# A three-term float32 product x + T[k] x: unit 0 in three pieces, the first x's fourth tile on SyncE's queue, new orders at the start

## The reference

```python
x:    (8, 512, 512)      # b, j, k
T:    (100, 512, 512)    # t, i, j
itok: (8,) int32         # 1 .. 98
Tb = T[itok - 1]
out = x + jnp.einsum('bij,bjk->bik', Tb, x)
```

## Time and profile before

| | us |
|---|---|
| median of three runs | 103.97 (103.88 to 104.11) |
| profiled execution | 104.08 |
| its span, first to last instruction | 102.3 |
| TensorE busy in the span | 96.1 (94%) |
| VectorE, GpSimd, ScalarE busy | 86.9, 72.7, 65.1 |
| matmuls of the three products (L452, L463, L474), each group | 34.5, 34.4, 33.2 |

### The profile page before, as it was taken

The page is one execution under the profiler, slowest core; times in us unless marked ns, Lnnn a source line. Parts: engine busy times, 40 slices in busy tenths (PEclk is TensorE's granted clock), DMA queues, the critical chain, the costliest instruction groups (busy, mean ns, idle before and its releaser), DMA issues.

```text
span 102.3 us, 1825 instructions
## 1 busy us (share of the span) xinstructions
PE 96.1 (94%) x440; PEld 80.1 (78%) x440; DVE 86.9 (85%) x100; ACT 65.1 (64%) x86; POOL 72.7 (71%) x38
## 2 busy tenths in 40 slices
PE   4996999999999999999999999999999999999950
PEld 4994888868888888888888888888888888888840
DVE  0165888999999999999999999999999999993250
ACT  0764669659578685858585859587785858452110
POOL 2000459999989799897979797979798998908100
PEclk9999999999999999999999999999999999999997
DMA  1899998996989889896999889998999330405064
GB/s 47 307 201 401 366 236 205 389 310 167 322 293 307 302 253 379 231 343 146 324 351 326 190 287 331 327 275 263 349 248 313 129 146 13 192 0 208 6 272 139
DMA packets 20749, 25.30 MB, mean 247 GB/s; under 512 B 2306, under 2 KB 16898, under 8 KB 19970
## 3 DMA queue, kind: packets, MB, share of 16 engines
q10 hardware_dynamic: 3602, 15.34, 41.7%
q1 hardware_dynamic: 17136, 9.84, 36.2%
HBM read 16.78 MB, written 8.39 MB: 246 GB/s over the span
## 4 chain that ended last, share of the span: by engine, by line
PE 88%; DMA 5%; SPq 2%; issue 0%; DVE 0%; ACT 0%
PE same L452 29%; PE same L463 28%; PE diff L474 28%; DMA T_sb<-T 5%; PE turned L437 1%; SPq L169 1%; PE diff L484 1%; PE turned L426 1%; PE same L484 0%; SPq L155 0%; DVE out_sb L409 0%; ACT TH_r L225 0%
## 5 line engine op out<-in xcount | busy, mean ns | idle before, releaser
L301 POOL TENSOR_TENSOR xL<-x_sb,xH 128x1024 fp32r<-128x1024 f32 x14 | 33.8, 2412 | 7.6 <-ACT xH L210 7.6
L317 POOL TENSOR_TENSOR TD_r<-TH_r,TL 128x1024 fp32r<-128x1024 f32 x14 | 33.8, 2413 | 2.9 <-issue 2.9
L452 PE MATMUL same<-xH,TH_r 128*128 128x512 f32 x128 | 34.5, 391 | 0.2 <-ACT TH_r L225 0.2
L463 PE MATMUL same<-xL,TL 128*128 128x512 f32 x128 | 34.4, 391 | 0.0
L474 PE MATMUL diff<-xD,TD_r 128*128 128x512 f32 x124 | 33.2, 390 | 0.1
L246 ACT ACTIVATE diff<-same 128x512 f32<-128x512 f32 x31 | 18.1, 582 | 22.8 <-PE same L463 22.8
L357 DVE STREAM_TRANSPOSE turned<-T_sb 128x512 f32<-128x512 f32 x28 | 29.2, 1089 | 0.0
L452 PEld LDWEIGHTS same<-xH,TH_r 128*128 128x128 f32 x128 | 23.9, 188 | 5.3 <-ACT TH_r L225 0.4
L463 PEld LDWEIGHTS same<-xL,TL 128*128 128x128 f32 x128 | 23.9, 188 | 4.9
L474 PEld LDWEIGHTS diff<-xD,TD_r 128*128 128x128 f32 x124 | 23.2, 188 | 5.2 <-issue 0.5
L385 DVE TENSOR_TENSOR out_sb<-x_sb,diff 128x512 f32<-128x512 f32 x31 | 20.9, 675 | 4.7 <-PE diff L474 4.7
(11 more groups left out here) (25 smaller groups left out, 21.6 us busy)
## 6 DMA issues: line engine op xcount, KB each, us to landing
out<-out_sb ACTq DMA_DIRECT2D x15, 512.0 KB, 5.2
T_sb<-T SPq DMA_DIRECT2D x112, 64.0 KB, 4.0
x_sb<-x ACTq DMA_DIRECT2D x6, 1024.0 KB, 6.6
x_sb<-x SPq DMA_DIRECT2D x2, 512.0 KB, 7.8
x_sb<-x ACTq DMA_DIRECT2D x2, 256.0 KB, 3.5
x_sb<-x ACTq DMA_DIRECT2D x1, 512.0 KB, 4.6
T_sb<-T SPq DMA_DIRECT2D x2, 256.0 KB, 5.6
T_sb<-T SPq DMA_DIRECT2D x1, 512.0 KB, 6.4
```

The source lines that it names most:

```text
L301: nc.gpsimd.tensor_tensor(half(xL, h), x_sb[b % X_SLOTS][:, i:i + 2], half(xH, h).bitcast(fp32), ALU.subtract).then_inc(xL_ready, 2)
L317: nc.gpsimd.tensor_tensor(TD_r[s][:], TH_r[s][:].bitcast(fp32), TL[s][:].bitcast(fp32), ALU.subtract).then_inc(TD_ready, 2)
L452: nc.tensor.matmul(same[U % 2][:], TH_r[p][:, i, j], xH[s][:, j], start=(j == 0), stop=False)
L463: done = nc.tensor.matmul(same[U % 2][:], TL[p][:, i, j], xL[s][:, j], start=False, stop=(j == N - 1))
```

## The change

Unit 0's transposed T, which stood in two pieces of two blocks (each with its own TH and TL cut), stands in three: block 0, block 1 and blocks 2 and 3. Block 1's piece goes into a free quarter of the bank `same[1]`. The first x is loaded in four transfers of one tile each instead of three; tiles 0 to 2 by ScalarE as before, and tile 3 by SyncE, behind T0 and ahead of T1. ScalarE cuts tile 3 behind the T cuts of unit 0, VectorE takes its low part behind the TL cuts. TensorE does unit 0's high and low products of blocks 0 to 2 around turn(1), and then the high and the low product with tile 3. Besides, ScalarE cuts half 2 of x before cut_T(3) instead of after it, VectorE's transposes of units 4 and 5 come before cut_T(3) and before sum_up(0), where they stood after sum_up(0), and WARM is 8 instead of 10.

```diff
--- before.py
+++ after.py
@@ -27,8 +27,7 @@
     RADIX = 4096.0
     LEAN = 1.0 - 0.5 / RADIX
     BY_PE = N
-    FIRST_X = [(0, 1), (1, 2), (2, 4)]
-    WARM = 10
+    WARM = 8
     HALVES = [slice(0, D // 2), slice(D // 2, D)]
 
     x_part = x.rearrange("b (p u) k -> b p u k", u=N)
@@ -61,20 +60,21 @@
         same = [ps(f"same{i}", [P, D]) for i in range(2)]
         diff = [ps(f"diff{i}", [P, D]) for i in range(2)]
 
-        first_halves = [(turned[:, 0, 0:2], slice(0, 2)), (turned[:, 1, 2:4], slice(2, 4))]
+        first_pieces = [(turned[:, 0, 0:1], slice(0, 1)), (same[1][:, P:2 * P].rearrange("p (j i) -> p j i", j=1), slice(1, 2)),
+                        (turned[:, 1, 2:4], slice(2, 4))]
 
         last_diff = [diff[(UNITS - 1) % 2], same[UNITS % 2]]
 
         eye_step = sem("eye_step")
         itok_loaded = sem("itok_loaded")
         x_loaded = [sem(f"x_loaded{s}") for s in range(X_SLOTS)]
-        first_x_loaded = [sem(f"first_x_loaded{i}") for i in range(len(FIRST_X))]
+        first_x_loaded = [sem(f"first_x_loaded{u}") for u in range(N)]
         half_x_loaded = [sem(f"half_x_loaded{i}") for i in range(2)]
         T_loaded = [[sem(f"T_loaded{s}_{n}") for n in range(N)] for s in range(T_SLOTS)]
         turned_by_pe = sem("turned_by_pe")
         turned_by_dve = sem("turned_by_dve")
-        first_half_turned = sem("first_half_turned")
-        first_half_TH_ready = sem("first_half_TH_ready")
+        first_piece_turned = sem("first_piece_turned")
+        first_TH_ready = sem("first_TH_ready")
         TH_ready = sem("TH_ready")
         TL_ready = sem("TL_ready")
         TD_ready = sem("TD_ready")
@@ -142,6 +142,9 @@
         def load_x(eng, b):
             eng.dma_start(x_sb[b % X_SLOTS][:], x_part[b]).then_inc(x_loaded[b % X_SLOTS], 16)
 
+        def load_first_x(eng, u):
+            eng.dma_start(x_sb[0][:, u], x_part[0, :, u]).then_inc(first_x_loaded[u], 16)
+
         def load_second_x(eng, i):
 
             eng.dma_start(x_sb[1][:, 2 * i:2 * i + 2], x_part[1, :, 2 * i:2 * i + 2]).then_inc(half_x_loaded[i], 16)
@@ -173,7 +176,9 @@
                 return sp.snap(t, min_val=0, max_val=K - 1)
 
             t = matrix(itok_row[0:1, 0:1])
-            load_T(sp, t, 0)
+            load_T(sp, t, 0, range(1))
+            load_first_x(sp, N - 1)
+            load_T(sp, t, 0, range(1, N))
             load_second_x(sp, 0)
             load_second_x(sp, 1)
             sp.wait_ge(itok_loaded, 16)
@@ -194,7 +199,7 @@
         @block.scalar
         def _(act):
             def cut_first_x(u):
-                act.wait_ge(first_x_loaded[min(u, 2)], 16)
+                act.wait_ge(first_x_loaded[u], 16)
                 nc.scalar.activation(xH[0][:, u], x_sb[0][:, u], COPY, scale=LEAN).then_inc(xH_ready, 1)
 
             def cut_x_half(h):
@@ -216,13 +221,13 @@
                 nc.scalar.activation(xH_copy[:], half(xH, h).bitcast(fp32), COPY).then_inc(xH_copied, 1)
 
             def cut_first_T():
-                for i, ready in enumerate((first_half_TH_ready, TH_ready)):
-                    bank, blocks = first_halves[i]
-                    if i == 0:
-                        act.wait_ge(first_half_turned, 1)
+                for i, (bank, blocks) in enumerate(first_pieces):
+                    if i < 2:
+                        act.wait_ge(first_piece_turned, i + 1)
                     else:
                         wait_turned(act, 1)
-                    nc.scalar.activation(TH_r[0][:, 0, blocks], bank, COPY, scale=LEAN / RADIX).then_inc(ready, 1)
+                    nc.scalar.activation(TH_r[0][:, 0, blocks], bank, COPY, scale=LEAN / RADIX
+                                         ).then_inc(first_TH_ready if i < 2 else TH_ready, 1)
 
             def cut_T(U):
                 wait_turned(act, U + 1)
@@ -249,18 +254,19 @@
                 for bank, cols in zip(last_diff, HALVES):
                     nc.scalar.activation(bank[:, cols], same[U % 2][:, cols], COPY, scale=-(RADIX + 1.0)).then_inc(seeded, 1)
 
-            for done, (u, end) in zip(first_x_loaded, FIRST_X):
-                act.dma_start(x_sb[0][:, u:end], x_part[0, :, u:end]).then_inc(done, 16)
+            for u in range(N - 1):
+                load_first_x(act, u)
             act.dma_start(itok_sb[:], itok_row).then_inc(itok_loaded, 16)
-            for u in range(N):
+            for u in range(N - 1):
                 cut_first_x(u)
             cut_first_T()
+            cut_first_x(N - 1)
             copy_xH_half(0)
             cut_T(1)
             seed(0)
             cut_T(2)
+            cut_x_half(2)
             cut_T(3)
-            cut_x_half(2)
             seed(1)
             copy_xH_half(2)
             cut_x_half(3)
@@ -359,9 +365,11 @@
                                     ).then_inc(turned_by_dve, 1)
 
             def cut_first_T():
-                for i, ready in enumerate((first_half_TH_ready, TH_ready)):
-                    bank, blocks = first_halves[i]
-                    dve.wait_ge(ready, 1)
+                for i, (bank, blocks) in enumerate(first_pieces):
+                    if i < 2:
+                        dve.wait_ge(first_TH_ready, i + 1)
+                    else:
+                        dve.wait_ge(TH_ready, 1)
                     cut = nc.vector.scalar_tensor_tensor(TL[0][:, 0, blocks], TH_r[0][:, 0, blocks].bitcast(fp32), -RADIX,
                                                          bank, ALU.mult, ALU.add)
                 cut.then_inc(TL_ready, 1)
@@ -385,19 +393,23 @@
                 nc.vector.tensor_tensor(out_sb[b % OUT_SLOTS][:, n], x_sb[b % X_SLOTS][:, n], diff[U % 2][:],
                                         ALU.subtract).then_inc(sum_ready, 1)
 
-            for u in range(N):
+            for u in range(N - 1):
                 first_xL(u)
             cut_first_T()
+            first_xL(N - 1)
             cut_x_half(0)
             cut_T(1)
             cut_x_half(1)
             cut_T(2)
+            turn(4)
             cut_T(3)
+            turn(5)
             sum_up(0)
             for k in range(1, PAIRS):
-                for p in T_pairs(k):
-                    turn(2 * p)
-                    turn(2 * p + 1)
+                if k > 1:
+                    for p in T_pairs(k):
+                        turn(2 * p)
+                        turn(2 * p + 1)
                 for h in xD_halves(k):
                     cut_x_half(h)
                 sum_up(2 * k - 1)
@@ -423,9 +435,10 @@
                 wait_T_loaded(pe, 0)
                 rows = T_sb[0][:, 0].rearrange("p (c j) -> p j c", j=N)
                 for j in range(N):
-                    done = nc.tensor.transpose(turned[:, j // 2, j], rows[:, j], eye[:])
-                    if j == 1:
-                        done.then_inc(first_half_turned, 1)
+                    bank, blocks = first_pieces[min(j, 2)]
+                    done = nc.tensor.transpose(bank[:, j - blocks.start], rows[:, j], eye[:])
+                    if j < 2:
+                        done.then_inc(first_piece_turned, 1)
                 done.then_inc(turned_by_pe, 1)
 
             def turn(U):
@@ -437,16 +450,30 @@
                     done = nc.tensor.transpose(turned[:, U % 2, j], rows[:, j], eye[:])
                 done.then_inc(turned_by_pe, 1)
 
+            def multiply_first(blocks, high):
+
+                for j in blocks:
+                    if high:
+                        if j < 2:
+                            pe.wait_ge(first_TH_ready, j + 1)
+                        else:
+                            pe.wait_ge(TH_ready, 1)
+                        pe.wait_ge(xH_ready, j + 1)
+                        nc.tensor.matmul(same[0][:], TH_r[0][:, 0, j], xH[0][:, j], start=(j == 0), stop=False)
+                    else:
+                        pe.wait_ge(TL_ready, 1)
+                        pe.wait_ge(first_xL_ready, j + 1)
+                        done = nc.tensor.matmul(same[0][:], TL[0][:, 0, j], xL[0][:, j], start=False, stop=(j == N - 1))
+                        if j == N - 1:
+                            done.then_inc(same_ready, 1)
+
             def multiply_high(U):
                 b, n = U // N, U % N
                 p, i, s = U // 2 % T_SETS, U % 2, b % X_SETS
                 if U >= 2:
                     pe.wait_ge(seeded, U - 1)
+                pe.wait_ge(TH_ready, U + 1)
                 for j in range(N):
-                    if U == 0 and j < 2:
-                        pe.wait_ge(first_half_TH_ready, 1)
-                    else:
-                        pe.wait_ge(TH_ready, U + 1)
                     if n == 0:
                         pe.wait_ge(xH_ready, b * N + j + 1)
                     nc.tensor.matmul(same[U % 2][:], TH_r[p][:, i, j], xH[s][:, j], start=(j == 0), stop=False)
@@ -456,9 +483,7 @@
                 p, i, s = U // 2 % T_SETS, U % 2, b % X_SETS
                 pe.wait_ge(TL_ready, U + 1)
                 for j in range(N):
-                    if n == 0 and b == 0:
```

(9 more changed lines are left out.)

## The result

The changed kernel is slower. Six runs gave a median of 105.71 us (105.24 to 106.53), the kernel before on the same chip 104.04 (103.49 to 104.4): a ratio of 1.0149, 95% interval 1.0105 to 1.0193. I had forecast 103.3. Its profiled execution took 106.53 us with a span of 104.4, so it is 0.8 us worse than the median, and what is read from it is on the high side.

A forecast was written before the change was run, and what follows sets the result against it. The kernel was taken as a fixed train of TensorE matmuls whose start is set by T0's landing, with GpSimd's line ending last. Only T0's 0.65 us counted, taking the median from 103.97 to 103.3 us; range 102.8 to 104.15.

The forecast's parts named there:

- T0 0.65 us earlier: T's first block, with 256 KB of x no longer ahead of it, lands at 7.7 instead of 8.36 us.
- T0 not earlier: Rival: T's first reads stay slow, T0 lands at 8.1 to 8.4; 103.8 to 104.1 us; chance 0.19.
- The ceiling of 0.8 us: DMA engines alternate between queues with work, so T0 gains only x's turns: at most an estimated 0.8 us.
- x3 at T0 + 0.65, T1 at 9.0 as before, since the bytes are the same.: On SyncE's queue, x's tile 3 lands at about 8.35 us and T1 still at 9.0 behind it.
- The start in three pieces: Unit 0 on TensorE: first product 0.23 us earlier, then a 0.2 us wait before turn(1).
- the low products end 0.25 us earlier: Unit 0's low products on TensorE end 3.4 us after T0 instead of 3.64.
- The second line: ScalarE - VectorE - GpSimd: TD(1) 0.5 us later, absorbed by GpSimd's 0.52 us idle; TD(3) ends at T0 + 14.5 as before.
- The new orders: ScalarE's earlier cut recovers GpSimd's idle time; VectorE's earlier transposes are covered, costing at most 0.3 us if not.
- The sum: TensorE's line gains 0.25 us after T0, GpSimd's 0.0; the later counts, leaving T0's own 0.65 us.
- x3 too late: Rival: ScalarE's in-order cut waits for tile 3, slower if it lands after 9.5; 104.4 to 104.8 us; chance 0.1.
- The second line isn't back: Rival: second x's first half lands after about 13.8, GpSimd's idle time isn't recovered; 103.7 to 104.3 us; chance 0.07.

The follow-up runs named there:

- T0_from_x: Kernel before, with T's first block read from x's batch 0 instead of T (that unit's product is of other data): 103.86 us, ratio 0.9954.
- two_tiles_ahead: Kernel before, with x's tiles 2 and 3 as one 512 KB transfer on SyncE's queue behind T0: 105.40 us, ratio 1.0111.
- td0_late: act_dve_old, with GpSimd's TD(0) made to wait until VectorE has done all four first_xL: 104.95 us, ratio 1.0055.
- pieces_act_new: Kernel before, with unit 0's three pieces (all four high products kept before turn(1)) and ScalarE's cut_x_half(2) ahead of cut_T(3): 103.47 us, ratio 0.9933.
- before_act_new: Kernel before, with ScalarE's new order alone, cut_x_half(2) ahead of cut_T(3): 104.02 us, ratio 0.9972.
- x3_on_act: Changed kernel, with x's tile 3 back on ScalarE's queue: 105.98 us, ratio 1.0146; repeated in a later set, 105.04 us, ratio 1.0070.
- act_dve_old: Changed kernel, with x's tile 3 back on ScalarE's queue and VectorE's transposes of units 4 and 5 back behind sum_up(0): 105.12 us, ratio 1.0099.
- dve_old: Changed kernel, with VectorE's transposes of units 4 and 5 back behind sum_up(0): 104.74 us, ratio 1.0029.
- act_td0_dve_new: x3_on_act, with GpSimd's TD(0) made to wait for VectorE's four first_xL; VectorE's new order stays: 104.53 us, ratio 1.0021.
- before_dve_new: Kernel before, with VectorE's new order alone, turn(4) ahead of cut_T(3) and turn(5) ahead of sum_up(0): 104.03 us, ratio 0.9992.
- old_orders: Changed kernel, with VectorE's and ScalarE's orders of before and 10 warm-up products: 104.96 us, ratio 1.0075.
- after_td0_late: Changed kernel, with GpSimd's TD(0) made to wait for VectorE's four first_xL: 105.62 us, ratio 1.0115.

## Why the prediction was wrong, point by point

**T0 0.65 us earlier.** The direction held and the size did not. From issue to landing T0 took 5.1 to 5.8 us in the five kernels with tile 3 behind it (median 5.3), and 5.0 to 6.9 in the eleven with all of x ahead (median 5.6; one of them is T0_from_x). The term measured about 0.3 us, inside a scatter of 1.9; with two tiles behind it T0 took 4.6 in the one execution that there is. The rival "T0 not earlier" describes the profiled execution. The ceiling of 0.8 us by the alternating queues (the Trainium skill, DMA: Bandwidth & Descriptors, Queues, rings and completion order) was respected, but it said nothing of why T's queue is slow while alone. The stretches 5 to 8 us of after (engines' busy times, then granted clock, DMA share, GB/s) show it:

```profile
5.00:6.00 1.00, 1.00 (x7) 1.00 (x7) 1.00 (x2) 0.57 (x2) 0.00 (x0) 1.00 0.47 96
6.00:7.00 1.00, 1.00 (x11) 1.00 (x11) 0.64 (x2) 0.61 (x1) 0.00 (x0) 1.00 0.90 123
7.00:8.00 1.00, 0.49 (x5) 0.30 (x3) 0.33 (x1) 0.00 (x0) 0.00 (x0) 1.00 0.90 289
```

and the same stretch of before:

```profile
5.00:6.00 1.00, 1.00 (x9) 1.00 (x9) 0.73 (x2) 0.62 (x1) 0.00 (x0) 1.00 0.90 270
```

Between 5 and 6 us T's queue had started and was slow, and x's last 0.2 MB had filled the DMA engines' time. With tile 3 taken out they were busy 47% of it.

What this term had wrong is the start of T's packets, which I kept at 5.0 to 5.2. Between 2 and 5 us T's queue (q1) moved nothing before, but this in after, and this in two_tiles_ahead:

```profile
q1 hardware_dynamic: 7, 0.01, 5.8%
...
q1 hardware_dynamic: 70, 0.14, 12.9%
```

By the packet records its first packet started at 4.84 to 5.61 us in the eleven executions with four tiles on ScalarE's queue (median 5.10), at 4.39 to 4.62 in the five with three (4.54), and at 3.89 with two, though T0 was issued at 2.8 to 3.0 in all of them. **So x's bytes did hold T back at its start, by about half a microsecond for one tile. What followed was no faster for it: the bytes that I took away had been filling time in which T's own stream was slow.** Why it is slow while alone isn't settled.

**"x3 at T0 + 0.65, T1 at 9.0 as before, since the bytes are the same."** This is the step that failed first. x3 landed at 9.55 (issued at 3.29, 6.26 us), T0 + 1.3, and T1 at 10.0 to 11.0 in all five kernels with tile 3 on SyncE's queue; 1.9 to 2.6 us behind T0, against 0.7 to 1.1 in the eleven with all of x on ScalarE's queue. Equal bytes in a queue are no equal time when the stream in front of them is slow for another reason. All that stood behind moved more than in proportion: the second x's halves to 14.3 and 16.5 (11.5 and 13.2 before), T4's last piece to 17.63 (14.30 before). T4's delay goes with that second half: in all 17 executions T4's fourth piece landed 1.0 to 1.2 us behind it, while in after the other three had landed by 15.02. T4's own issue isn't the cause. With tile 3 on ScalarE's queue T4's first piece was issued at 7.7 to 8.4 as well, and the fourth landed at 14.3 to 16.0. No kernel here issues T4 ahead of the second x, so whether that would have saved it is open. I had also counted the issue at 0.45 us and seen it as covered. The issue of the second x's two halves took 1.89 us instead of 1.03, and T4's followed at 7.86 instead of 6.47. SyncE's queue, of after:

```profile
4.81 1.89 SPq L150 DMA_DIRECT2D x_sb<-x  x2
7.86 2.37 SPq L162 DMA_DIRECT2D T_sb<-T  x5
```

and of before:

```profile
4.29 1.03 SPq L147 DMA_DIRECT2D x_sb<-x  x2
6.47 3.58 SPq L159 DMA_DIRECT2D T_sb<-T  x7
```

The halves' issue took 1.7 to 2.4 us in all six kernels with a transfer more on this queue, 0.9 to 1.3 in the eleven others.

**The start in three pieces.** Right in its parts, wrong in its end: first product 0.23 us earlier (9.09 - 8.34 = 0.75 after the first transpose, 0.98 before), and TensorE waits 0.22 us before turn(1) when T1 is there, as predicted; in the changed kernel T1's lateness made it 0.97. But "the low products end 0.25 us earlier" didn't come, not even with T1 and the port out of the way: turn(2), which stands behind them, starts 3.49 us after the first transpose in td0_late and 3.42 in before. That wait, and a fifth product between turn(1) and turn(2), use up the gain; I had set my 3.4, worked out step by step, against a 3.64 from the chain, which counts ends another way. The sum didn't hang on it. pieces_act_new kept the fourth product as the cover, and gained 0.23 us over before_act_new.

**The second line.** "0.5 us later, and 0.5 of idle time to take it" had the mechanism right and left out the larger cost. ScalarE's slide was nearly as said (the copy at 10.11 against 9.50, 1.8 us after T0 instead of the 1.66 that I had said, and xH(3)'s cut waited 0.1 for its tile), and GpSimd ran from TD(1) into xL without idle time. But I let first_xL(3) keep its 0.69 us from the rows of before, where GpSimd had nothing to do yet. It moved beside TD(0) and took 1.63 to 1.82. TD(1) started 6.6 us after T0 instead of the 5.9 that I had said, and TD(3) ended at T0 + 15.1 instead of 14.5. With T1 on time TensorE waited for this instruction directly too, 0.3 us before its low product with tile 3 (x3_on_act, act_dve_old). A page of the Trainium skill that I had not weighed states this rule, SBUF — State Buffer, SBUF: two separate sides: VectorE and GpSimd share one pair of ports, held for a whole instruction, and when an instruction of VectorE with two SBUF inputs meets one of GpSimd that reads SBUF, the later of the two waits. The traces agree: TD(0) started first, by 0.01 to 0.19 us, and 1.82 us is 1.29 of GpSimd and the rest. And VectorE's xD with one input in PSUM took 1.21 us beside GpSimd (at 18.37 in before), no more than elsewhere.

**The new orders: "all covered; if the covers fail, their price is at most the 0.3 of TL."** Wrong by a factor of five, and the largest part of the loss. I priced turn(4) with a T4 landed by 13.9 (its fourth piece was issued at 8.23, not by 7.7, and landed at 14.30) and didn't ask what is queued behind it if it comes late. In the changed kernel it stood 2.33 us waiting; behind it were cut_T(3), turn(5) and sum_up(0), for which seed(2) waits (2.9 us), for which diff(2) waits, and TL of units 4 and 5. TensorE lost 1.0 us before diff(2) (0.8 of it is in the list of waits) and 0.3 at TL, and the trace is 1.6 us longer than that of dve_old. That it takes both, late T4 and new order, is shown from three sides: the order with T4 on time is free (act_td0_dve_new 89.90, before_dve_new 90.02), late transfers with the old order cost 0.0 to 0.1 (dve_old and old_orders against act_dve_old, all three with the port's delay), and the two together cost 1.6 (after against dve_old).

**The sum.** On TensorE the 2.2 us of the changed kernel can be followed product by product, each counted from the first transpose and set against before. The first product is 0.2 earlier. Behind turn(1), which waits for T1, TensorE is 0.9 late; before diff(2) it loses 1.0 more, and 0.3 at TL of units 4 and 5. The port's delay isn't in this sum: TD(3) ended at 23.39, and diff(3) started at 25.18. It lies beside T1's wait, and each hides the other, so that taking out the port alone (after_td0_late) or the queue alone (dve_old against act_dve_old) changes little in the traces. Only with the order of before is the port's delay what counts, 0.6 us; the late T4 through VectorE's new order then makes the step from 90.61 to 92.23. By the clock the first of these steps is 0.3 us (dve_old against the kernel before; the interval reaches from 0 to 0.6) and the second 1.0 to 1.2.

**The rivals.** "x3 too late" was close in kind, with its turning point at a landing after 9.5. x3 came at 9.55, which by that formula costs under 0.1 us. "The second line isn't back" had the right transfer: its condition, the second x's first half landing after about 13.8, came true at 14.3. But the price that it named wasn't paid, since GpSimd found that half cut and had no idle time. What cost was T1 and T4 in the same late stream, T4 with VectorE's whole list queued behind it, and that none of my rivals had. The range ended at 104.15, and by my own text the slower cases held only 0.14.

## What to carry to other kernels

Moving a transfer later moves everything behind it on that queue, issues and data, and often by more than its bytes at full rate; look whether the bytes that you take out of the way were in the way or were filling idle DMA engines. When two delays lie side by side, taking out one shows nothing; take out both before you call either harmless. Before pulling an instruction forward in an in-order engine, price the case that its operand comes late, with all that is now queued behind it: an early place is free only when the data are early too. And when an instruction moves, look at what other engines run at its new time; a duration from the old place is no price.

## What the runs showed of the hardware that I had not expected

- VectorE's subtraction of two SBUF tiles (128x512, 0.69 us alone) takes 1.63 to 1.82 us beside a GpSimd instruction of 1.29 us on SBUF tiles that started first, and ends 0.55 us behind it in all six traces.
- One and the same 256 KB transfer, T0, landed 5.0 to 6.9 us after its issue in ten executions (of ten kernels, all with x's four tiles on ScalarE's queue). That this is most of the scatter between runs is likely but not shown, since only profiled executions tell T0.
- T's first packet starts the later the more of x is on the other queue: 3.89 us with two tiles, 4.4 to 4.6 with three, 4.8 to 5.6 with four.
- With six instead of five transfers issued by SyncE in a row at the start, the issue of the last two takes 1.7 to 2.4 us instead of 0.9 to 1.3. What it waits for isn't shown.
- Four transfers of 256 KB instead of two and one of 512 KB for the first x cost 0.5% (0.1 to 1.0%), with nothing to be seen in the profile.
